# Layer 0's routed experts: the last 48 inner rows stacked with their rests, and the down projection one step later

## The reference, cut to what matters

```python
h = silu(einsum('td,efd->etf', x, W1)) * einsum('td,efd->etf', x, W3)   # 16 experts, 176 inner rows each
routed = einsum('etf,edf->td', h * combine.T[:, :, None], W2)           # down to 256 columns
out = shared + routed
```

## Time and profile before

| | |
|---|---|
| time, 3 runs | 1277.73 us median, 1275.62 to 1278.14 |
| the profiled execution | 1278.45 us, its span 1276.6 us |
| PE busy over the span | 983.0 us (77%) |
| DVE, ACT, POOL busy | 749.2, 632.4, 486.4 us |
| mean granted TensorE clock | 0.867 of full speed |
| routed stage, first and last y on ACT | 551.23 and 740.41 us |

### The profile page before, as it was taken

The page is one execution under the profiler, slowest core; times in us unless marked ns, Lnnn a source line. Parts: engine busy times, 40 slices in busy tenths (PEclk is TensorE's granted clock), DMA queues, the critical chain, the costliest instruction groups (busy, mean ns, idle before and its releaser), DMA issues. The chain is left out here.

```text
span 1276.6 us, 21259 instructions
## 1 busy us (share of the span) xinstructions
PE 983.0 (77%) x5454; PEld 815.6 (64%) x5454; DVE 749.2 (59%) x1828; ACT 632.4 (50%) x1658; POOL 486.4 (38%) x645
## 2 busy tenths in 40 slices
PE   5367698999997778778999912797679942999990
PEld 2255587888885656568999912675567731888870
DVE  3754498999984855465444417984465542343433
ACT  0244698999982354365565513696322212333330
POOL 2334464666650477013444423765063320000005
PEclk8677798999997888888999965999789965999995
DMA  5235533333312424274333346000531003010104
GB/s 199 64 130 170 166 86 92 92 89 90 93 31 88 158 101 167 77 231 138 117 118 118 109 173 214 1 1 1 161 110 64 17 29 103 21 31 26 33 14 136
DMA packets 111889, 123.08 MB, mean 96 GB/s; under 512 B 46792, under 2 KB 85320, under 8 KB 111552
## 3 DMA queue, kind: packets, MB, share of 16 engines
q1 hardware_dynamic: 103408, 99.07, 26.0%
q0 software_dynamic: 8400, 23.01, 5.0%
HBM read 77.72 MB, written 44.32 MB: 96 GB/s over the span
## 5 line engine op out<-in xcount | busy, mean ns | idle before, releaser
L662 ACT ACTIVATE PR<-PS,nmax 128x128 f32<-128x128 f32 (+3 forms) x256 | 135.7, 552 | 9.9 <-DVE nmax L703 8.7
L580 POOL TENSOR_SCALAR PR<-PR,rinv 128x128 f32<-128x128 f32 (+3 forms) x256 | 131.5, 532 | 0.0
L703 DVE TENSOR_REDUCE nmax<-PS 128x1 f32<-128x128 f32 (+3 forms) x256 | 113.9, 483 | 24.8 <-PE PS L606 19.5
L1297 POOL DMA_INDIRECT r_results<-r_y,r_to x79 | 75.8, 960 | 134.8 <-DVE r_to L1348 105.8
L711 DVE TENSOR_TENSOR PTlo<-PS,PThi 128x512 fp32r<-128x512 f32 (+1 forms) x192 | 103.3, 593 | 2.9 <-ACT PThi L672 2.9
L672 ACT ACTIVATE PThi<-PS 128x512 fp32r<-128x512 f32 (+1 forms) x192 | 96.8, 545 | 12.4 <-PE PS L618 12.4
L2180 POOL DMA_INDIRECT x_yg<-x_results,d_slots x16 | 18.2, 1135 | 197.1 <-DMA x_results<-x_y 192.5
L605 PE MATMUL PS<-K,Q 128*128 128x128 f32 (+3 forms) x256 | 84.6, 390 | 10.3 <-PEq L259 5.6
L618 PE MATMUL PS<-ident,PR 128*128 128x128 f32 x640 | 87.6, 283 | 3.6 <-DVE PTlo L711 3.0
L634 PE MATMUL PS<-PThi,V 128*128 128x512 f32 (+3 forms) x256 | 86.1, 349 | 3.8 <-DMA V<-v_parts 2.8
L2233 DVE TENSOR_TENSOR x_h<-PS,x_sg 128x256 f32<-128x256 f32 x68 | 28.9, 425 | 92.9 <-ACT x_sg L2202 92.9
(11 more groups left out here) (357 smaller groups left out, 3122.2 us busy)
## 6 DMA issues: line engine op xcount, KB each, us to landing
r_xg<-r_sorted SPq DMA_DIRECT2D x79, 129.0 KB, 2.1
r_wst<-in_routed SPq DMA_DIRECT2D x16, 608.0 KB, 4.8
K<-k_parts SPq DMA_DIRECT2D x128, 64.0 KB, 1.8
c_yg<-r_results SPq DMA_DIRECT2D x16, 512.0 KB, 7.7
v_parts<-vp SPq DMA_DIRECT2D x4, 1024.0 KB, 4.4
Q<-q_parts SPq DMA_DIRECT2D x64, 64.0 KB, 1.8
Q<-q_parts SPq DMA_DIRECT2D x128, 32.0 KB, 1.7
V<-v_parts SPq DMA_DIRECT2D x64, 64.0 KB, 2.0
```

The costliest lines, as they stand in the source:

```text
L580: pool.tensor_scalar(PR[:, e % 4, i, 0:w], PR[:, e % 4, i, 0:w], rinv[:, e % 4, i:i + 1], 1.0, ALU.mult, ALU.mult).then_inc(norm_done, 1)
L662: act.activation(PR[:, e % 4, i, 0:w], k.PS[:, i, 0:w], ACT.Exp, bias=nmax[:, e % 4, i:i + 1], accum_out=rsum[:, e % 4, i:i + 1]).then_inc ...
L703: dve.tensor_reduce(nmax[:, e % 4, i:i + 1], k.PS[:, i, 0:P * (i + 1)], AX_X, ALU.max, negate=True).then_inc(max_done, 1)
L1297: pool.indirect_dma_start(out=d.results, out_offset=bass.IndirectOffsetOnAxis(ap=to[:, i % TO_LANES:i % TO_LANES + 1], axis=0), in_=y[:, i ...
```

## The change: what it does

The down projection's second half has 48 rows in use. The change puts two copies of them in the 128 rows: `times` writes the last 48 columns of `h` a second time, 64 columns further on, and the weights' last 48 rows are laid out twice as well. After the transposition, `hlo`'s second half is the rest in all rows; the new ACT stage `stack` copies the rounded values from `hhi` over rows 0 to 63. One operand then holds rounded values above and rests below, and two matmuls (by `wlo` and by `whi`) give what three gave, with the product of rest and `wlo` added. `down` and `result` go from lag 3 to lag 4, `down` is issued ahead of `rows` in a step, `result` ahead of `split_h`, and `stack` (lag 3) is the second stage in an ACT step. `h_done` counts two for each block. The three numbers of lanes are as they were.

```diff
--- before.py
+++ after.py
@@ -27,6 +27,7 @@
 X_LANES, Y_LANES, TO_LANES = 8, 3, 12
 
 W_LANES = 3
+HALF = P // 2
 
 NOWHERE = 65536.0
 L1_EXPERTS, L1_FF = 2, 1024
@@ -1246,19 +1247,21 @@
         xg, xhi, xlo = sb("xg", [X_LANES, ROW]), sb("xhi", [2, D], F32R), sb("xlo", [2, D], F32R)
         sg, h = sb("sg", [2, L0_FF]), sb("h", [2, 2 * P])
         hhi, hlo = sb("hhi", [2, 2 * P], F32R), sb("hlo", [2, 2 * P], F32R)
+
+        REST = L0_FF - P
         y, to, spare = sb("y", [Y_LANES, D]), sb("to", [TO_LANES], I32), sb("spare", [Y_LANES])
         S = lambda s: k.sem("r_" + s)
         w_in, w_hi, w_done = weights.w_in, S("w_hi"), S("w_done")
         x_in, xT_ready, xhi_done, xlo_done = [S(f"x_in{i}") for i in range(X_LANES)], S("xT_ready"), S("xhi_done"), S("xlo_done")
-        up_ready, sg_done, h_done, hT_ready, hhi_done, hlo_done = (
-            S("up_ready"), S("sg_done"), S("h_done"), S("hT_ready"), S("hhi_done"), S("hlo_done"))
+        up_ready, sg_done, h_done, hT_ready, hhi_done, hlo_done, stacked = (
+            S("up_ready"), S("sg_done"), S("h_done"), S("hT_ready"), S("hhi_done"), S("hlo_done"), S("stacked"))
         y_ready, y_done, to_done, zeroed = S("y_ready"), S("y_done"), S("to_done"), S("zeroed")
         block = c.enter_context(nc.Block())
         PS_UP, PS_X, PS_H, PS_Y = (lambda s: k.PS[:, s % 2, 0:UP], lambda s: k.PS[:, 2 + s % 2, 0:D],
                                    lambda s: k.PS[:, 4 + s % 2, 0:2 * P], lambda s: k.PS[:, 6 + s % 2, 0:D])
 
         def steps(*stages):
-            for at in range(-3, N + 4):
+            for at in range(-3, N + 5):
                 for lag, stage in stages:
                     if 0 <= at - lag < N:
                         stage(at - lag)
@@ -1313,20 +1316,24 @@
 
             def silu(s):
                 act.wait_ge(up_ready, s + 1)
-                wait(act, h_done, s - 1)
+                wait(act, h_done, 2 * (s - 1))
                 act.activation(sg[:, s % 2, :], PS_UP(s)[:, 0:L0_FF], ACT.Silu).then_inc(sg_done, 1)
 
             def split_h(s):
                 act.wait_ge(hT_ready, s + 1)
                 wait(act, y_ready, s - 1)
                 act.activation(hhi[:, s % 2, :], PS_H(s), ACT.Copy).then_inc(hhi_done, 1)
+
+            def stack(s):
+                act.wait_ge(hlo_done, s + 1)
+                act.activation(hlo[0:HALF, s % 2, P:2 * P], f32(hhi[0:HALF, s % 2, P:2 * P]), ACT.Copy).then_inc(stacked, 1)
 
             def result(s):
                 act.wait_ge(y_ready, s + 1)
                 if s >= Y_LANES:
                     act.wait_ge(d.y_out[s % Y_LANES], 16 * (s // Y_LANES))
                 act.activation(y[:, s % Y_LANES, :], PS_Y(s), ACT.Copy, scale=xg[:, s % X_LANES, D:D + 1]).then_inc(y_done, 1)
-            steps((-3, split_weights), (-2, block_hi), (0, silu), (2, split_h), (3, result))
+            steps((-3, split_weights), (3, stack), (-2, block_hi), (0, silu), (4, result), (2, split_h))
 
         @block.vector
         def _(dve):
@@ -1351,10 +1358,15 @@
             def times(s):
                 dve.wait_ge(sg_done, s + 1)
                 wait(dve, hT_ready, s - 1)
+                if s == 0:
+                    dve.wait_ge(zeroed, 2)
                 dve.tensor_tensor(h[:, s % 2, 0:L0_FF], PS_UP(s)[:, L0_FF:UP], sg[:, s % 2, :], ALU.mult).then_inc(h_done, 1)
+                dve.tensor_tensor(h[:, s % 2, P + HALF:P + HALF + REST], PS_UP(s)[:, L0_FF + P:UP], sg[:, s % 2, P:L0_FF],
+                                  ALU.mult).then_inc(h_done, 1)
 
             def split_h(s):
                 dve.wait_ge(hhi_done, s + 1)
+                wait(dve, y_ready, s - 1)
                 dve.tensor_tensor(hlo[:, s % 2, :], PS_H(s), f32(hhi[:, s % 2, :]), ALU.subtract).then_inc(hlo_done, 1)
             steps((-3, split_weights), (-2, block_lo), (0, times), (2, split_h), (0, destination))
 
@@ -1375,7 +1387,7 @@
                     pe.wait_ge(w_done, s + 1)
                 expert[s] = pe.value_load(d.expert[0:1, s:s + 1], min_val=0, max_val=E - 1)
                 pe.wait_ge(xlo_done, s + 1)
-                wait(pe, h_done, s - 1)
+                wait(pe, h_done, 2 * (s - 1))
                 for m in range(DM):
                     cols = slice(m * UP, (m + 1) * UP)
                     last = split3_moving(pe, PS_UP(s), xhi[:, s % 2, m * P:(m + 1) * P], xlo[:, s % 2, m * P:(m + 1) * P],
@@ -1385,22 +1397,20 @@
             def rows(s):
                 if s == 0:
                     pe.wait_ge(zeroed, 2)
-                pe.wait_ge(h_done, s + 1)
+                pe.wait_ge(h_done, 2 * (s + 1))
                 wait(pe, hlo_done, s - 1)
                 pe.transpose(PS_H(s)[:, 0:P], h[:, s % 2, 0:P], k.ident[:])
                 pe.transpose(PS_H(s)[:, P:2 * P], h[:, s % 2, P:2 * P], k.ident[:]).then_inc(hT_ready, 1)
 
             def down(s):
-                pe.wait_ge(hlo_done, s + 1)
+                pe.wait_ge(stacked, s + 1)
                 wait(pe, y_done, s - 1)
                 e = expert.pop(s)
-                for part in range(2):
-                    cols = slice(DM * UP + part * D, DM * UP + (part + 1) * D)
-                    f = slice(part * P, (part + 1) * P)
-                    last = split3_moving(pe, PS_Y(s), hhi[:, s % 2, f], hlo[:, s % 2, f],
-                                         moving(whi, e, cols), moving(wlo, e, cols), part == 0, part == 1)
-                last.then_inc(y_ready, 1)
-            steps((-2, columns), (0, up), (2, rows), (3, down))
+                first, rest = (slice(DM * UP + part * D, DM * UP + (part + 1) * D) for part in range(2))
+                split3_moving(pe, PS_Y(s), hhi[:, s % 2, 0:P], hlo[:, s % 2, 0:P], moving(whi, e, first), moving(wlo, e, first), True, False)
+                pe.matmul(PS_Y(s), hlo[:, s % 2, P:2 * P], moving(wlo, e, rest), start=False, stop=False)
+                pe.matmul(PS_Y(s), hlo[:, s % 2, P:2 * P], moving(whi, e, rest), start=False, stop=True).then_inc(y_ready, 1)
+            steps((-2, columns), (0, up), (4, down), (2, rows))
 
 
 class ConvWeights:
@@ -2352,6 +2362,7 @@
     routed[:, :, :DM * 2 * L0_FF] = pairs.reshape(L0_EXPERTS, P, DM * 2 * L0_FF)
     downs = np.zeros((L0_EXPERTS, 2 * P, D), np.float32)
     downs[:, :L0_FF] = a["L0_ffn_W2"].transpose(0, 2, 1)
+    downs[:, P + HALF:HALF + L0_FF] = downs[:, P:L0_FF]
     routed[:, :, DM * 2 * L0_FF:] = downs.reshape(L0_EXPERTS, 2, P, D).transpose(0, 2, 1, 3).reshape(L0_EXPERTS, P, 2 * D)
     o["routed0"] = routed
```

## The result

The changed kernel takes 1362.4 us (median of four runs, 1359.5 to 1372.5) against 1276.7 us for the kernel before (four runs, 1274.4 to 1278.1). The ratio is 1.069, with a 95% interval of 1.066 to 1.071: slower by 86 us. The forecast was 1365 us, range 1330 to 1393. The profiled execution of the changed kernel is the longest of its four, 1372.5 us with a span of 1370.7, so differences read between the two traces add up to 94 us, not 86.

The account below looks back on a forecast made before the run. TensorE was taken as the bound once weights have arrived, with 0.6 us of slack in the block buffers' ring. Terms 49.7 + 26.3 + 2 + 1 + 8 = 87 us on 1277.7 gave 1365 us, range 1330 to 1393.

Parts of the forecast that it names:

- Two steps instead of three between y and the block's load: Steady routed steps: two steps take 6.14 us, one 3.07 against 2.12 before; +49.7 us, saved matmul included.
- the signs: Changed profile: `columns` waits 0.4 to 1.2 us in nearly all steps, PE near 70% busy, routed stage ends near 828 us.
- Weights behind blocks: Steps while expert weights arrive, experts 8 to 15: 7.57 us a step instead of 3.82, +26.3 us over seven steps.
- Expert 8 itself: Weights' steps: expert 8 comes about one early step late, +2 us by estimate.
- The clock: Steady steps: TensorE at 1.2 GHz about 22% of the time, +8 us, bounds 0 and 49.
- The read of the number: PE, between a `columns` that waited and `up`: if the expert's number's read is hidden, 0.6 us a pair, 19 us, comes off.
- `stack` and the second product hidden: Steady steps: `stack` takes 0.2 us within ACT's 0.77 us of waiting; the second product, 0.2 us, is hidden on DVE.
- the block ring: Block buffers, y to transfer, landing, `columns` and next y: 6.14 us for two steps; with the weights' ring, 85%.
- the third rival: ACT and VectorE become a ring of their own, 1.95 us a step; about 1277 us, no change, 2%.
- A matmul less is 7.5 us if PE stays the bound: Down projection: one matmul less saves 0.12 us a step, 7.5 us over 64 steady steps, 9.3 over all 79 blocks.
- the rival at 1269: Steady steps: the block buffers' ring doesn't bind and the saved matmul shows, weights cost nothing; 1269 us, 3%.
- the tail: End of the routed stage: 82 steps instead of 81, the last ones short chains of ACT, DVE and PE; +1 us.

Follow-up runs that it names:

- the early release: Changed kernel with VectorE copying the weight column out of the block, so SP's next load no longer waits for y: 1255.0 us, ratio 0.982.

## Why the prediction was right, point by point

*Two steps instead of three between y and the block's load.* Right, and shown from three sides: the early release takes the loss away (1255.0), one buffer less in the old code makes it (1382.5), and the old distance with the new code gives the old time (1274.4). The pair of steps was worked out as 6.14 us and is 6.11 in the undisturbed rows above. The terms hold one by one: issue 0.79 for 0.85, landing and start of `columns` 2.14 for 2.1, wait to `up` 0.85.

*Not every step waits.* The sum left open whether one parity slips behind the other, and the signs named waits in nearly all steps. PE's record shows 28 waits in some 55 steps: one parity does slip behind. The other signs are near: PE is busy for 72% of the steady stretch, and the last y starts at 836 us where 828 was forecast.

*Weights behind blocks.* Right in kind. Seven steps were to grow by 3.75 us each, 26.3 in all; from 559.45 to 615.73 us, the splits of experts 8 and 15 in the changed kernel's trace, it is 8.04 a step and 29.5 us. The undisturbed step is 7.76, since the weights took 4.37 us to their split (579.72 to 584.09) instead of 4.14, and two landed more than 5 us after their start. Expert 8 itself came 3.4 us later than before, where I had estimated 2: its split stands 28.5 us after that of expert 0, and stood 25.1 after it. Together this part grew by 33 us, from 51.8 to 84.8. Put ahead of the block, the weights gave 35 us back and the part took 50.0.

*The clock.* The term was 8 us for the steady part, at 22% of the time at 1.2 GHz. From 617 to 827 us the granted clock is 0.94, so about 12% at the low level. It came differently from what I wrote: at the full clock through most of it, with the low level at or right behind each of the six longest waits. PE's timeline at one of these:

```profile
692.81 0.27 PE L1403 MATMUL PS<-ident,r_h 128*128 128x128 f32 x1
695.57 0.44 PE L1382 MATMUL PS<-ident,r_xg 128*128 128x128 f32 x2 [2.49 <-DMA r_xg<-r_sorted]
696.65 0.66 PE L2334 MATMUL PS<-r_wlo,r_xhi 128*128 x1 [0.64 <-issue]
697.11 0.49 PE L2335 MATMUL PS<-r_whi,r_xlo 128*128 x1
697.40 0.49 PE L2336 MATMUL PS<-r_whi,r_xhi 128*128 x1
```

After 2.5 us without work the matmuls stand 0.29 us apart instead of 0.16, and this pair takes over 9 us. SP's timeline has the start of the transfer that PE waited for, 4.1 us ahead of `columns`, where 2.1 is usual:

```profile
691.46 0.33 SPq L1281 DMA_DIRECT2D r_xg<-r_sorted  x1
```
 y of step 12 starts at 617.51 and of step 76 at 826.51, so a step is 3.27 on average; less 3.06 this is 13 us for late blocks and clock together. An estimate of how they share it: five of the steps behind a wait have matmuls at the low level and last 3.75 to 4.38 us from `columns` to `columns`, where 2.71 is usual, 6.8 us in all. So the term of 8 was of the right size, for a reason that was only half right. The rule of the Trainium skill that I weighed ("TensorE: Matmul & The Clock Gate", HAM oscillation) fits the usual step better than my reading of the earlier trace rows did: waits of some 1.1 us behind longer work left the clock up. In the weights' steps, at 0.57 in the first row of the windows view of the changed kernel, PE stands idle twice a step, for 1.3 to 2.1 us, between 1.9 and 3.0 us of work at the low level; the rule has the wait longer than the work, which isn't so here. It is about waits that come in every step. One late block is another case: the 2.5 us at 695.57 came behind 5.6 us of work with no idle time over 0.5, and the clock fell all the same.

*The read of the number, 0.6 us a pair.* Right: 0.65.

*`stack` and the second product hidden.* Right: 0.20 us of ACT, as assumed, and a duration of 0.29 where the estimate from the budget was 0.41. Nothing of it is in the time while the block ring is longer. The ring of the third rival can't be over 1.98 us at lag 4, since steps of 1.98 ran with it in place; 1.95 was worked out. At lag 3 there is such a ring of 2.58 us, because it holds `down`.

*A matmul less is 7.5 us if PE stays the bound.* Wrong, though it decided nothing here: the step of the prediction that priced it by its distance of 0.12 us (the first part of the change, and with it the rival at 1269). Taken out by itself it gave 0.5 us, with stacking 4.2 us and overlapping intervals. A step has a floor near 2.1 us in PE's program of reads and addresses, which the prediction didn't look for.

*Luck in the last figure.* The forecast of 87 us and the measured 86 are closer than the terms. In the trace the weights' part grew by 33 us where 28.3 was forecast, the steady steps by 62.2 where 57.7 was, clock included, and the tail by 0.1 instead of 1: 94 us with the small rest outside these. The three other executions are 8 to 13 us shorter than the profiled one, and which part is shorter in them is not known.

## What to carry to other kernels

A stage moved one step later lengthens the life of every buffer that its last reader holds. Count, for each ring of buffers, the steps from the last read to the next use, and set issue, landing and the engines' passes against them: with eight buffers there was 0.6 us of slack in three steps, which late transfers used up now and then already, and the change took a step of 2.1. Ask also what the last reader needs; here it was one column of 258, and copying it away gave 18 us in the old kernel, where stacking on top of it gave 4. And before an instruction is taken out of a busy engine, look whether its own issue has a floor just below.

## What was not expected of the hardware

The place of one instruction can matter much or not at all: with the read of a register from memory in PE's program moved ahead of `columns`, the time changes by 0.9 us or less while PE doesn't wait for blocks, and 0.65 us is gained behind each wait. PE busy for 70 of 70 us hid a floor near 2.1 us a step in PE's other instructions. And a block's transfer, 2.1 us to its landing in the median, took up to 3.9 in the changed kernel, and up to 4.1 to the `columns` that waited for it in the pair shown above. There it cost its own lateness and a pass at 1.2 GHz. Why single transfers land late stays open.
